# Decoder layer on one core: cross-attention keys and queries stacked per slot in 48 rows, two row tiles

## The chip, the cores and the metric

One core of a Trainium2 chip. The metric is the device time of one launch in microseconds (us). Three runs of the kernel before took 3350.82, 3353.17 and 3353.92 us, a median of 3353.17. The profiled execution took 3353.8 us, of which 3352.1 us are the span from the first instruction to the last.

## The reference, cut to what matters

A pre-norm decoder layer on 16 sequences of 128 tokens and 1024 features, fp32: self-attention, cross-attention over a context, feed-forward.

```python
x = x + attn(layernorm(x)); x = x + xattn(layernorm(x), ctx, ctx); x = x + ffn(layernorm(x))
# xattn: H = 16 heads, M = 4 superposed slots, dk = 16, projections of 1024 x 1024
scores = einsum('bhqdm,bhkdm->bhqkm', qh, kh) / sqrt(dk)
weights = softmax(scores, axis=3)
out = einsum('bhqkm,bhkdm->bhqdm', weights, vh)
```

There are 64 (head, slot) pairs. Each has its own score matrix over the 128 tokens of a sequence, with a contraction over only 16 features.

## The kernel before, in words

The layer runs in three phases, one after the other. The change is in the second, `cross_attention_phase` (L906). It goes over 4 blocks of 512 tokens (4 tiles of 128, a tile is one sequence) and, in each, over 8 groups of 128 projected features. A group holds 8 slots of 16 features. That makes 32 groups; they are software-pipelined in 33 steps: a step projects keys, queries and values of group n (`pieces`, 24 chunks of three matmuls of 128x512 in fp32r, a high and a low part of each operand) and does attention for group n-1.

The order of TensorE's work is written out by hand at the end of `step`: `scores(0)` first, the other three `scores(t)` between the pieces, with `turn_probs(t)` (transposes of the probabilities, L1261), `mix_values(t)` (L1281) and `project(t, half)` among them. The result of the projection stays in two banks and is split on ScalarE and VectorE into a high and a low half (`kh`, `kl`, `qh`, `ql`).

Scores need fp32 accuracy from fp32r operands: q·k is taken as qh·kh + qh·kl + ql·kh. For this the three products are put under one another in the contraction rows. Halves go out to HBM (`k_parts`, `q_parts`) and come back in another layout, all on SyncE's DMA queue: `stack_keys(a, part)` and `stack_queries(a, part)` (L1048 to L1056) for a = 0, 1, 2. Four pairs of slots (r = 0..3) each get a tile of 96 rows: 3 parts x (2 slots x 16 features). Keys lie block-diagonally: `kstack[96, pair, w, token]` holds slot w's 16 rows of each part in half w and zeros (a memset on GpSimd, once, L1143) in the other. Queries lie dense in `qstack[96, pair, token]`. One matmul (L1249) then gives both slots of a pair:

```python
ins = nc.tensor.matmul(s_ps[:, r * 2 * P:(r + 1) * 2 * P], qstack[:, r, t * P:(t + 1) * P],
                       kstack[:, r, :, t * P:(t + 1) * P], start=True, stop=True)
```

So `scores(t)` is 4 matmuls of 96 x 128 weights and 256 moving columns. `s_ps` spans two banks of 512 columns. After it VectorE takes the maximum per slot (L1512), ScalarE the exponentials in two halves of 4 slots (L1403), VectorE sums and inverses, GpSimd multiplies (L1163).

SyncE's order within a step: weights of the next group's first unit, `kh` to HBM, `kl` to HBM; then a wait for the last `scores` of the step (L1100, because `kstack` and `qstack` are single buffers) and for the landing of `kh`; `stack_keys(0)`; wait for `qh`, store it; `stack_keys(2)`; wait for `ql`, store it; `stack_keys(1)`; `stack_queries(0)`, `stack_queries(1)`; wait for the landing of `ql`; `stack_queries(2)`; then the weights of the second unit. Each `stack_keys` is two DMAs of 16 partitions and 128 KB, each `stack_queries` one DMA of 32 partitions and 256 KB. `scores(0)` of the next step waits for all nine (L1246, L1247).

The self-attention phase has two small TensorE blocks that matter as rows of comparison: L634 and L649. L649 (`mix_values` there) uses 32-row operands at partitions 0, 32, 64 and 96 in turn: 16 matmuls with 32 x 128 weights and 128 moving columns, plain fp32, of which the trace shows 32 in each of 32 blocks. L1281 in the cross-attention phase uses 128 x 32 weights with four output row groups, plain fp32.

Of the kernel before, what the change touches and what calls it, by code (L numbers as in the profile page):

```python
# [8 lines left out]
F32R = mybir.dt.float32r  # L9
# [4 lines left out]
P = 128  # L14
# [5 lines left out]
BT = TILES * P  # L20
# [16 lines left out]
DK = 16  # L37
# [8 lines left out]
def f32(ap):  # L46
    return ap.bitcast(F32)
# [858 lines left out]
def cross_attention_phase(nc, sems, ident, bias_qkv, eps, x1, ctxT, w_folded_hi, w_folded_lo, wo, k_parts, q_parts,  # L906
# [13 lines left out]
    PC = P // PAIRS  # L920
    PARTS = 3
    KSTACK = 16 * PARTS * 2
    QSTACK = 16 * PARTS
    STEPS = [CrossStep(n) for n in range(BLOCKS * CH + 1)]


# [7 lines left out]
    with ExitStack() as ctx:  # L934
        def sb(name, shape, dt=F32):
            return ctx.enter_context(nc.sbuf_tensor(name, shape, dt))
# [16 lines left out]
        kl = sb("ca_kl", [P, BT], F32R)  # L953
        qh = sb("ca_qh", [P, BT], F32R)
        ql = sb("ca_ql", [P, BT], F32R)
        kstack = sb("ca_kstack", [PARTS * PC, PAIRS, 2, BT], F32R)
        qstack = sb("ca_qstack", [PARTS * PC, PAIRS, BT], F32R)
        vT = sb("ca_vT", [P, BT])
        v = sb("ca_v", [P, TILES * PAIRS, VW])
        probs = sb("ca_probs", [P, 2, SLOTS, P])  # L960
# [67 lines left out]
        def _(sp):  # L1028
# [16 lines left out]
                    sp.wait_ge(c_split, b * KC + k)  # L1045
                sp.dma_start(raw_context(b, k), tile_of(ctxT, b * KC + k)).then_inc(c_loaded[k // 2], 16)

            def stack_keys(a, part):  # L1048
                by_slot = part.rearrange("(r w d) n -> w d r n", w=2, d=DK)
                for w in range(2):  # L1050
                    rows = slice(a * PC + w * DK, a * PC + (w + 1) * DK)
                    sp.dma_start(f32(kstack[rows, :, w]), by_slot[w]).then_inc(k_stacked, 16)

            def stack_queries(a, part):
                sp.dma_start(f32(qstack[a * PC:(a + 1) * PC]), part.rearrange("(r p) n -> p r n", p=PC)
                             ).then_inc(q_stacked, 16)  # L1056

            def store_x2(s, t):

# [16 lines left out]
            for s in STEPS:  # L1076
# [10 lines left out]
                if s.proj:  # L1087
                    sp.wait_ge(ow_split, s.n + 1)
                    sp.dma_start(owraw[:], tile_of(wo, s.g)).then_inc(owraw_loaded, 16)
                    next_weights(s, 0)  # L1090
                    sp.wait_ge(u_hi, s.n * 2 + 1)
                    sp.dma_start(k_parts[0], f32(kh[:])).then_inc(k_hi_stored, 16)
                    sp.wait_ge(u_free, s.n * U + 3)
                    sp.dma_start(k_parts[1], f32(kl[:])).then_inc(k_lo_stored, 16)
                    if after_closing:
                        load_acc(s.b, 1)
                        load_acc(s.b, 2)
                        load_acc(s.b, 3)
                    if s.attn:
                        sp.wait_ge(s_done, s.m * TILES + TILES)  # L1100
                    else:
                        sp.wait_ge(cleared, 1)
                    sp.wait_ge(k_hi_stored, s.n * 16 + 16)
                    stack_keys(0, k_parts[0])
                    sp.wait_ge(u_hi, s.n * 2 + 2)
                    sp.dma_start(q_parts[0], f32(qh[:])).then_inc(q_hi_stored, 16)
                    stack_keys(2, k_parts[0])
                    sp.wait_ge(u_free, s.n * U + 4)
                    sp.dma_start(q_parts[1], f32(ql[:])).then_inc(q_lo_stored, 16)
                    sp.wait_ge(k_lo_stored, s.n * 16 + 16)  # L1110
                    stack_keys(1, k_parts[1])
                    sp.wait_ge(q_hi_stored, s.n * 16 + 16)
                    stack_queries(0, q_parts[0])
                    stack_queries(1, q_parts[0])
                    sp.wait_ge(q_lo_stored, s.n * 16 + 16)
                    stack_queries(2, q_parts[1])
                    next_weights(s, 1)
# [22 lines left out]
        @block.gpsimd  # L1140
        def _(pool):
            pool.sem_inc(ow_split, 1)
            nc.gpsimd.memset(f32(kstack[:]), 0.0).then_inc(cleared, 1)  # L1143
            nc.gpsimd.memset(v[:], 0.0).then_inc(cleared, 1)

            def out_weights(s):
# [31 lines left out]
        def _(pe):  # L1178
# [19 lines left out]
            def step(s):  # L1198
# [42 lines left out]
                def scores(t):  # L1241
                    if not s.attn:
                        return
                    if t == 0:
                        pe.wait_ge(k_stacked, n * KSTACK)
                        pe.wait_ge(q_stacked, n * QSTACK)  # L1246
                    pe.wait_ge(exp_done, (m * TILES + t) * 2 + 2)  # L1247
                    for r in range(PAIRS):
                        ins = nc.tensor.matmul(s_ps[:, r * 2 * P:(r + 1) * 2 * P], qstack[:, r, t * P:(t + 1) * P],  # L1249
                                               kstack[:, r, :, t * P:(t + 1) * P], start=True, stop=True)  # L1250
                    ins.then_inc(s_done, 1)

                def turn_probs(t):
# [10 lines left out]
                def mix_values(t):  # L1264
# [12 lines left out]
                    pe.wait_ge(o_split, m * TILES + (t + 1))  # L1277
                    for w in range(2):
                        for r in range(PAIRS):
                            j = 2 * r + w  # L1280
                            ins = nc.tensor.matmul(o_ps[DP * r:DP * (r + 1), 0:P],  # L1281
                                                   v[:, t * PAIRS + r, DP * w:DP * (w + 1)],
                                                   probsT[:, j * P:(j + 1) * P], start=(w == 0), stop=(w == 1))
# [185 lines left out]
        def _(dve):  # L1469
# [10 lines left out]
            def step(s):  # L1480
# [19 lines left out]
                def place_v():  # L1500
                    if not s.attn:
                        return
                    dve.wait_ge(cleared, 2)
                    dve.wait_ge(v_turned, n)
                    nc.vector.tensor_copy(v[:].rearrange("p r (w x) -> p (r w) x", w=2)[:, :, 0:DK],
                                          t_ps[:, 0:BT].rearrange("p (s d) -> p s d", d=DK)).then_inc(v_placed, 1)
# [523 lines left out]
```

## Time and profile before

| | |
|---|---|
| profiled execution | 3353.8 us |
| its span | 3352.1 us |
| TensorE matmul busy | 3207.4 us, 96% |
| weight loads busy | 2580.7 us, 77% |
| VectorE, ScalarE, GpSimd busy | 42%, 36%, 49% |
| cross-attention scores (L1249) | 512 matmuls, 90.2 us busy, 17.5 us idle before them |
| DMA to `ca_kstack` | 192 of 128 KB, 3.4 us from issue to landing |
| DMA to `ca_qstack` | 96 of 256 KB, 5.4 us from issue to landing |

Matmuls are pipelined: one is recorded for 0.39 us while the next starts 0.23 us later. So the cost of a stretch of TensorE work is read from start to start, not from the durations. PE is the matmul, PEld the load of its weights. "[x <-issue]" behind a row is idle time of x us before it that ended when a wait in TensorE's own sequencer did.

### The profile page before, as it was taken

The page shows a single profiled execution, that of the slowest core. Times are in us where ns is not written, and L with a number is a line of the kernel's source. Part 1 is how long each engine was busy: PE and PEld are TensorE (multiplying, and loading weights), DVE is VectorE, ACT ScalarE, POOL GpSimd, SP SyncE. Part 2 cuts the span into 40 slices and gives each one's busy share as a digit, 9 for nine tenths or more (in the row PEclk, how much of TensorE's full clock was granted, in tenths as well). Part 3 has the DMA queues.
Part 4 walks back from the last instruction along what each step waited for, and adds up shares of the span by engine and source line. Part 5 has one row for each costly group of instructions (what it writes and reads, how often), then busy time and mean ns, then how long its engine had stood idle before and what let it go on. Part 6 is the DMA issues. An engine that isn't in the chain of part 4 may idle for free. (4 is left out here: it accounts for less than half of the span.)

```text
span 3352.1 us, 48808 instructions
## 1 busy us (share of the span) xinstructions
PE 3207.4 (96%) x18212; PEld 2580.7 (77%) x18212; DVE 1410.9 (42%) x2264; ACT 1210.5 (36%) x2433; POOL 1641.5 (49%) x1032
## 2 busy tenths in 40 slices
PE   7999999999999999999999969999999999998999
PEld 6777777778777777788888747777777777776787
DVE  3232242222242223233232235676666666664453
ACT  3233242232232322333333225565555555552100
POOL 4767667677676676765445333333333333331000
PEclk9999999999999999999999979999999999998999
DMA  5333344333344433435445256768768777765142
GB/s 190 101 119 114 124 138 146 119 114 105 126 131 147 131 103 116 144 101 201 150 133 162 93 208 213 230 200 256 219 204 254 232 211 246 236 189 206 66 143 76
DMA packets 176885, 536.23 MB, mean 160 GB/s; under 512 B 21704, under 2 KB 21832, under 8 KB 176728
## 3 DMA queue, kind: packets, MB, share of 16 engines
q1 hardware_dynamic: 174424, 525.65, 49.4%
q10 hardware_dynamic: 2304, 8.39, 0.6%
q8 instruction: 110, 1.80, 0.2%
q14 instruction: 47, 0.39, 0.0%
HBM read 433.29 MB, written 100.66 MB: 159 GB/s over the span
## 5 line engine op out<-in xcount | busy, mean ns | idle before, releaser
L53 PE MATMUL sa_u<-sa_ln_xh,sa_wh 128*128 128x512 f32 x1536 | 610.0, 397 | 38.0 <-POOL sa_wl L513 33.6
L54 PE MATMUL sa_u<-sa_ln_xl,sa_wh 128*128 128x512 f32 x1536 | 599.8, 390 | 0.0
L55 PE MATMUL sa_u<-sa_ln_xh,sa_wl 128*128 128x512 f32 x1536 | 599.1, 390 | 0.0
L513 POOL TENSOR_TENSOR sa_wl<-sa_wraw,sa_wh 128x1024 fp32r<-128x1024 f32 x192 | 459.9, 2400 | 170.3 <-ACT sa_wh L701 170.3
L563 POOL TENSOR_TENSOR sa_pl<-sa_praw,sa_ph 128x1024 fp32r<-128x1024 f32 x128 | 320.8, 2536 | 430.0 <-ACT sa_ph L755 430.0
L1163 POOL TENSOR_TENSOR ca_probs<-ca_probs,ca_inv 128x512 f32<-128x512 f32 x256 | 266.8, 1051 | 538.2 <-DVE ca_inv L1530 538.1
L850 DVE TENSOR_TENSOR sa_acc<-sa_pr,sa_acc 128x512 f32<-128x512 f32 x256 | 176.9, 691 | 774.5 <-PE sa_pr L55 774.5
L53 PE MATMUL sa_pr<-sa_ph,sa_oh 128*128 128x512 f32 x1024 | 403.0, 394 | 4.7 <-POOL sa_pl L563 4.4
L54 PE MATMUL sa_pr<-sa_pl,sa_oh 128*128 128x512 f32 x1024 | 404.2, 395 | 0.0
L55 PE MATMUL sa_pr<-sa_ph,sa_ol 128*128 128x512 f32 x1024 | 398.8, 389 | 0.0
L53 PEld LDWEIGHTS sa_u<-sa_ln_xh,sa_wh 128*128 128x128 f32 x1536 | 289.0, 188 | 114.2 <-POOL sa_wl L513 44.2
L55 PEld LDWEIGHTS sa_u<-sa_ln_xh,sa_wl 128*128 128x128 f32 x1536 | 289.1, 188 | 61.3
L54 PEld LDWEIGHTS sa_u<-sa_ln_xl,sa_wh 128*128 128x128 f32 x1536 | 289.4, 188 | 56.9
L719 ACT ACTIVATE sa_qT<-sa_u 128x512 f32<-128x512 f32 x128 | 76.5, 597 | 627.4 <-PE sa_u L55 627.4
L1403 ACT ACTIVATE ca_probs<-ca_s,ca_negtop 128x128 f32<-128x128 f32 x1024 | 286.7, 384 | 4.1
L842 DVE TENSOR_TENSOR sa_ol<-sa_s,sa_oh 128x512 fp32r<-128x512 f32 x32 | 22.1, 691 | 508.2 <-ACT sa_oh L767 508.2
L53 PEld LDWEIGHTS sa_pr<-sa_ph,sa_oh 128*128 128x128 f32 x1024 | 192.9, 188 | 50.4 <-POOL sa_pl L563 4.7
L55 PEld LDWEIGHTS sa_pr<-sa_ph,sa_ol 128*128 128x128 f32 x1024 | 192.8, 188 | 43.1
L54 PEld LDWEIGHTS sa_pr<-sa_pl,sa_oh 128*128 128x128 f32 x1024 | 193.2, 189 | 38.7
L701 ACT ACTIVATE sa_wh<-sa_wraw 128x1024 fp32r<-128x1024 f32 x192 | 202.0, 1052 | 17.8 <-DMA sa_wraw<-in_wqkv 17.8
L1521 DVE TENSOR_REDUCE ca_total<-ca_probs 128x4 f32<-128x512 f32 x256 | 172.7, 674 | 80.6 <-ACT ca_probs L1403 77.0
L1545 DVE TENSOR_TENSOR ca_acc<-ca_x,ca_acc 128x512 f32<-128x512 f32 x224 | 154.9, 691 | 122.3 <-PE ca_x L55 114.5
(215 smaller groups left out, 5778.8 us busy)
## 6 DMA issues: line engine op xcount, KB each, us to landing
sa_wraw<-in_wqkv SPq DMA_DIRECT2D x192, 512.0 KB, 3.7
sa_praw<-in_wproj SPq DMA_DIRECT2D x128, 512.0 KB, 3.7
three_wh<-w_folded_hi SPq DMA_DIRECT2D x96, 512.0 KB, 5.8
three_wl<-w_folded_lo SPq DMA_DIRECT2D x96, 512.0 KB, 6.8
ca_kstack<-k_parts SPq DMA_DIRECT2D x192, 128.0 KB, 3.4
ca_qstack<-q_parts SPq DMA_DIRECT2D x96, 256.0 KB, 5.4
ca_owraw<-in_wo SPq DMA_DIRECT2D x32, 512.0 KB, 3.8
sa_raw<-in_w_turned SPq DMA_DIRECT2D x24, 512.0 KB, 6.5
```

Source lines behind the costliest of these rows:

```text
L53: nc.tensor.matmul(out, ah, bh, start=(first and i == 0), stop=False)
L54: nc.tensor.matmul(out, ah, bl, start=False, stop=False)
L55: ins = nc.tensor.matmul(out, al, bh, start=False, stop=(last and i == len(parts) - 1))
L513: nc.gpsimd.tensor_tensor(wl[:, u % 3], wraw[:, u % 3], f32(wh[:, u % 3]), ALU.subtract).then_inc(w_split, 1)
L563: nc.gpsimd.tensor_tensor(pl[:, h], praw[:, h], f32(ph[:, h]), ALU.subtract).then_inc(p_split, 1)
L701: nc.scalar.activation(wh[:, u % 3], wraw[:, u % 3], ACT.Copy).then_inc(w_hi, 1)
L719: nc.scalar.activation(dst[u], u_ps[u % 2][:], ACT.Copy).then_inc(u_copied, 1)
L850: nc.vector.tensor_tensor(part, pr_ps[half][:], part, ALU.add).then_inc(pr_free, 1)
L1163: nc.gpsimd.tensor_tensor(probs[:, t % 2, js], probs[:, t % 2, js], inv[:, t % 2, js].unsqueeze(2).broadcast_to([P, SH, P]), ALU.mult).the ...
L1403: ins = nc.scalar.activation(probs[:, t % 2, j], s_ps[:, j * P:(j + 1) * P], ACT.Exp, scale=CROSS_SCALE, bias=negtop[:, j:j + 1])
L1521: nc.vector.tensor_reduce(total[:, t % 2, js], probs[:, t % 2, js], AX.X, ALU.add).then_inc(total_done, 1)
L1545: nc.vector.tensor_tensor(part, pr_bank(t, half)[:], part, ALU.add).then_inc(x_free, 1)
```

## The change

Keys and queries of each slot get 48 rows of their own (3 parts x 16 features): slot w of a pair sits at partitions 64w to 64w + 47, in `kstack` and in `qstack`. The zeros and their memset go, with SyncE's wait for it. A score matmul is one slot: 48 x 128 weights, 128 moving columns, from partition 0 or 64, with even slots written to the first bank of `s_ps` and odd ones to the second. There are 8 of them in a `scores(t)` in place of 4. `stack_queries` becomes two DMAs of 16 partitions and 128 KB, as the keys already have it; the keys' two keep number and size and write 8 KB in one piece per partition. The slot order in `s_ps` and behind it is all even, then all odd.

```diff
-    QSTACK = 16 * PARTS
+    QSTACK = 16 * PARTS * 2
+    ROWS = PARTS * DK
+    SLOT_TILE = 64
...
-        kstack = sb("ca_kstack", [PARTS * PC, PAIRS, 2, BT], F32R)
-        qstack = sb("ca_qstack", [PARTS * PC, PAIRS, BT], F32R)
+        kstack = sb("ca_kstack", [SLOT_TILE + ROWS, PAIRS, BT], F32R)
+        qstack = sb("ca_qstack", [SLOT_TILE + ROWS, PAIRS, BT], F32R)
...
-            def stack_keys(a, part):
+            def stack(dst, a, part, stacked):
                 by_slot = part.rearrange("(r w d) n -> w d r n", w=2, d=DK)
                 for w in range(2):
-                    rows = slice(a * PC + w * DK, a * PC + (w + 1) * DK)
-                    sp.dma_start(f32(kstack[rows, :, w]), by_slot[w]).then_inc(k_stacked, 16)
+                    rows = slice(w * SLOT_TILE + a * DK, w * SLOT_TILE + (a + 1) * DK)
+                    sp.dma_start(f32(dst[rows]), by_slot[w]).then_inc(stacked, 16)
+
+            def stack_keys(a, part):
+                stack(kstack, a, part, k_stacked)

             def stack_queries(a, part):
-                sp.dma_start(f32(qstack[a * PC:(a + 1) * PC]), part.rearrange("(r p) n -> p r n", p=PC)
-                             ).then_inc(q_stacked, 16)
+                stack(qstack, a, part, q_stacked)
...
-                    else:
-                        sp.wait_ge(cleared, 1)
...
-            nc.gpsimd.memset(f32(kstack[:]), 0.0).then_inc(cleared, 1)
...
                     for r in range(PAIRS):
-                        ins = nc.tensor.matmul(s_ps[:, r * 2 * P:(r + 1) * 2 * P], qstack[:, r, t * P:(t + 1) * P],
-                                               kstack[:, r, :, t * P:(t + 1) * P], start=True, stop=True)
+                        for w in range(2):
+                            rows = slice(w * SLOT_TILE, w * SLOT_TILE + ROWS)
+                            j = w * PAIRS + r
+                            ins = nc.tensor.matmul(s_ps[:, j * P:(j + 1) * P], qstack[rows, r, t * P:(t + 1) * P],
+                                                   kstack[rows, r, t * P:(t + 1) * P], start=True, stop=True)
...
-                            j = 2 * r + w
+                            j = w * PAIRS + r
```

## Rows read from the trace of the kernel before

**Rows 1.** Stretch: us, busy of PE, PEld, DVE, ACT, POOL; clock, DMA share, GB/s.
```profile
2018.00:3050.00 1032.00, 1010.17 (x6808) 795.43 (x6808) 686.57 (x1223) 569.05 (x1558) 371.66 (x311) 0.98 0.72 222
```

**Rows 2.** Groups by line of TensorE: busy, mean ns, idle before and what ended it.
```profile
L1249 PE MATMUL ca_s<-ca_kstack,ca_qstack 96*128 96x256 f32 x512 | 90.2, 299 | 17.5 <-issue 13.8 <-ACT ca_probs L1403 3.4
```

**Rows 3.** Timeline of PE, second step's scores(1), scores(2), scores(3): start, us, what.
```profile
2025.83 0.39 PE L55 MATMUL ca_u<-halves_h,three_wl 128*128 128x512 f32 x1
2026.05 0.64 PE L1249 MATMUL ca_s<-ca_kstack,ca_qstack 96*128 96x256 f32 x4
2026.53 0.40 PE L53 MATMUL ca_u<-halves_h,three_wh 128*128 128x512 f32 x1
2026.77 0.40 PE L54 MATMUL ca_u<-halves_l,three_wh 128*128 128x512 f32 x1
...
2031.54 0.74 PE L1249 MATMUL ca_s<-ca_kstack,ca_qstack 96*128 96x256 f32 x4
2032.12 0.40 PE L53 MATMUL ca_u<-ca_ln_xh,three_wh 128*128 128x512 f32 x1
...
2035.57 1.03 PE L1261 MATMUL ca_t<-ident,ca_probs 128*128 128x128 f32 x8
2036.36 0.72 PE L1249 MATMUL ca_s<-ca_kstack,ca_qstack 96*128 96x256 f32 x4
2036.92 0.40 PE L53 MATMUL ca_u<-halves_h,three_wh 128*128 128x512 f32 x1
```

**Rows 4.** Timeline of PE, one block of L649 between full-array matmuls.
```profile
1537.53 0.39 PE L55 MATMUL sa_u<-sa_ln_xh,sa_wl 128*128 128x512 f32 x1
...
1537.86 0.37 PE L649 MATMUL sa_vt<-sa_probsT,sa_v 32*128 32x128 f32 x1
...
1538.08 0.27 PE L649 MATMUL sa_vt<-sa_probsT,sa_v 32*128 32x128 f32 x1
...
1538.75 0.27 PE L649 MATMUL sa_vt<-sa_probsT,sa_v 32*128 32x128 f32 x1
1538.95 0.50 PE L53 MATMUL sa_u<-sa_ln_xh,sa_wh 128*128 128x512 f32 x1
1539.29 0.40 PE L54 MATMUL sa_u<-sa_ln_xl,sa_wh 128*128 128x512 f32 x1
```

**Rows 5.** Timeline of SP, the stacking behind ql of step 29: start, us, DMAs issued.
```profile
2913.99 0.42 SPq L1109 DMA_DIRECT2D q_parts<-ca_ql  x1
2914.46 0.92 SPq L1052 DMA_DIRECT2D ca_kstack<-k_parts  x2
2915.42 2.38 SPq L1055 DMA_DIRECT2D ca_qstack<-q_parts  x3
```

**Rows 6.** By tile, the DMAs of rows 5: ca_kstack x2, ca_qstack x3.
```profile
DMA to landing us min/median/max: 3.9/4.2/4.4
...
DMA to landing us min/median/max: 5.0/5.3/5.8
```

**Rows 7.** Stretches, columns as in rows 1: keys' pair, then queries, in that queue.
```profile
2917.25:2919.25 2.00, 2.00 (x14) 1.73 (x13) 0.69 (x1) 0.42 (x1) 0.00 (x0) 1.00 1.04 167
2919.50:2921.25 1.75, 1.75 (x21) 1.07 (x21) 0.81 (x2) 0.63 (x2) 0.00 (x0) 1.00 1.06 206
```

**Rows 8.** Timeline of PE: scores(0) behind the stacking of steps 29, 26 and 18.
```profile
2923.55 0.64 PE L1249 MATMUL ca_s<-ca_kstack,ca_qstack 96*128 96x256 f32 x4
...
2829.58 0.71 PE L1249 MATMUL ca_s<-ca_kstack,ca_qstack 96*128 96x256 f32 x4 [1.23 <-issue]
2830.13 0.39 PE L53 MATMUL ca_u<-ca_ch,three_wh 128*128 128x512 f32 x1
...
2571.16 0.71 PE L1249 MATMUL ca_s<-ca_kstack,ca_qstack 96*128 96x256 f32 x4 [1.67 <-issue]
```

**Rows 9.** Stretches, columns as in rows 1: behind the waits of 1.23 and 1.67 us.
```profile
2829.50:2833.00 3.50, 3.42 (x19) 2.98 (x20) 1.32 (x2) 1.38 (x6) 0.00 (x0) 1.00 1.04 410
2572.00:2575.30 3.30, 3.30 (x9) 2.51 (x8) 1.83 (x2) 2.10 (x9) 0.00 (x0) 0.50 1.03 420
```

More of the change, by code:

```diff
@@ L1502, in place_v @@
                         return
-                    dve.wait_ge(cleared, 2)
+                    dve.wait_ge(cleared, 1)
                     dve.wait_ge(v_turned, n)
```

## The prediction

> **What bounds the kernel now.** I read the page first (TensorE busy in 37 of 40 slices), then the stretch of the phase that changes: 1010 of 1032 us of it have a matmul in flight, so TensorE's stream sets the time [rows 1]. What it does beside streaming stands in the groups by line: 17.5 us idle before the scores, 3.4 of them on ScalarE in the last step, 13.8 on TensorE's own wait [rows 2]. The timeline places these at `scores(0)`, where the stacked keys and queries must have landed: 5.7 us in the first step and 8.1 us over eight later ones, two of which stand in [rows 8]. VectorE, ScalarE and GpSimd are busy 67%, 55% and 36% of the phase and nothing there is late but in the last step. So two things can move the time: the length of the four score blocks of a step, and the moment at which the last stacking DMA lands.
>
> **The score blocks on TensorE.** A block of four matmuls between full-array work costs, from the last L55 before it to the L54 behind it, 2026.77 - 2025.83 = 0.94 us [rows 3]; without a block that would be two starts of 0.23, so 0.48 us for four matmuls.
>
> The new block has eight matmuls in two row tiles. The trace has no block of two tiles, the nearest is L649 with four [rows 4]. Its 32 matmuls are eight rounds of four, one in each tile; the rows show the last tile of the rounds. From L55 to it 0.33 (0.10 above the usual 0.23); 0.22 to the second round (its weights can't be loaded ahead); then 0.67 for six rounds, 0.11 each; 0.20 from the last to L53; 0.34 from L53 to L54, 0.11 above the usual. Eight matmuls in two tiles are four rounds: 0.22 + 0.11 + 0.11 = 0.44 from first to last. Sum: 0.33 + 0.44 + 0.20 + 0.34 = 1.31, less 0.01 for two tiles fewer in a round, 1.30, against 0.94, so **+0.36 us** for a block between full-array matmuls. That is `scores(1)`, and `scores(0)` where it doesn't wait. Where it waits the entry is hidden: behind a wait the block now takes 0.55 to L53 [rows 8] and 0.23 on; it would take 0.44 + 0.01 + 0.20 + 0.34 = 0.99, so +0.21.
>
> `scores(2)` stands behind `mix_values`, itself a tiled block, and pays 0.58 to L53 today, not 0.48 [rows 3]: some of the change of tiling is paid already. 0.58 + 0.23 = 0.81 becomes 0.99: +0.18. `scores(3)` stands behind the transposes, 0.79 + 0.56 + 0.24 = 1.59 from the first of them to L54 [rows 3]; with the same 0.99 and an entry between 0 and 0.17 more I take 0.30 (0.19 to 0.36).
>
> A step: 0.21 + 0.36 + 0.18 + 0.30 = 1.05 us; 32 times: **+33 us**. All of it is on the path, since TensorE has no slack elsewhere in a step. Bounds: if entry and exit cost nothing, four rounds of 0.11 = 0.44 against 0.48, -0.04 x 128 = -5 us. If the two tiles didn't run side by side, eight times the 0.10 of a transpose with the same loads and columns (0.79 for eight, [rows 3]) makes 0.79 for 0.44: another 0.35 x 128 = +45, together +78. I take L649's own figures, since block and surroundings are alike; its plain fp32 is the one difference that speaks for the lower end.
>
> **The stacking.** The keys' six DMAs a step stay. The queries' three of 256 KB become six of 128 KB, with three issues more on SyncE at some 0.45 us [rows 5]. Behind them in that queue come the weights of the second unit, and the input tile or raw context; their first use is the ninth piece, behind eight pieces of three starts of 0.23 us [rows 3], 5.5 us after `scores(0)`, so 1.4 us later costs nothing. The queue is already backlogged there: the last query waits for the landing of `ql`, is issued at 2917.5 and lands 5.3 later, at 2922.8 [rows 5, 6]; 0.73 us on `scores(0)` starts unhindered [rows 8]. So in that backlog `ql` lands at 2917.5, the pair of keys (issued at 2914.5 and 2914.9) at 2918.3 and 2919.4, the queries at 2920.4, 2921.7 and 2922.8. So 256 KB as two DMAs of 16 partitions took 1.9 us and as one of 32 partitions 1.0 to 1.3. By rate the difference is smaller: 167 against 206 GB/s [rows 7]. The new queries are like the keys' pair. By the rate 786 KB take 4.7 us and not 3.8: +0.9. By the landings three pairs of 1.9 against 3.5: +2.2; but that 1.9 starts from the landing of a store in HBM and holds the difference between two kinds of landing, so the value is nearer to the rate. I take **+1.2 us**. Bounds: +2.2, and below nothing the rate that the same queue reaches with weights, 420 GB/s [rows 9], where 786 KB take 1.9 us, so -1.9.
>
> A block of scores(3) that ends 0.18 us later against what follows it (0.20 + 0.34 behind its last matmul, for 0.12 + 0.24) gives the chain 0.2 us back, because all of the chain hangs on `scores(3)`: the keys wait for it, and `qh` is drained behind its exponentials. So queries land 1.0 us later against TensorE. Read as in rows 5, 6 and 8, the 32 steps have these margins between landing and `scores(0)`: none in 12 steps (it waits already), 0.1 to 0.8 with mean 0.44 in 17, 1.3 to 1.6 in the three at a block's end. 12 x 1.0 + 17 x (1.0 - 0.44) = **+22 us**.
>
> Longer waits can cost the clock. Behind 1.23 us of waiting the granted clock stayed at 1.00, behind 1.67 it was 0.50 for 3.3 us [rows 8, 9], which is 1.2 and not 2.4 GHz and gave up half of that, 1.7 us. Of the new waits only two cross from one to the other (0.86 and 1.23, in steps 22 and 26, plus 1.0); the many of 1.0 to 1.3 don't: **+3 us**.
>
> The rule that bears on the stacking: the Trainium skill, "SBUF — State Buffer", Door 1, says that a transfer's rate goes with the ports that its partitions reach, four ports for 16 partitions at 27 GB/s each, and that partitions 32 apart share a port while 64 apart don't. Partitions 0 to 31 and 32 to 63, the first two query DMAs of today, then share eight ports, which gives 1.2 us each and agrees with the 1.2 measured; the new pairs reach the other half too. By that rule six in flight could use all sixteen and need 1.8 us instead of 3.5, or, one after another, 7.2. Which it is hangs on how many run at once, and no row shows it for halves 64 apart.
>
> **Cheap edits.** The memset on GpSimd (3.5 us once, at the start) and SyncE's wait for it lie beside the first projections; they are worth nothing. Slot order: the reduce, the exponentials and the copies keep their shapes, so nothing.
>
> **Sum.** 3353.8 (profiled execution) + 33 + 22 + 3 = 3412; it stands 0.6 above the median, so **3411 us**, 1.7% slower.
>
> **Rivals.**
> First, *the queries land no later* (0): only the blocks count. 3353 + 33 less some 2 of the present waits: 3384. For it: the rate of 167 is a short stretch, and six DMAs may spread better than two. Against it: the landings.
>
> Second, *they land sooner* by up to 1.9 us, because the two halves go to different parts of the memory: the 8.1 us of later waits go, with them two dips of the clock (3.4, that of [rows 9] and one behind a wait of 3.2 us), and 1.8 in the first step; the blocks cost 3 more, since `scores(0)` waits nowhere. 3353 + 36 - 13 = 3376. The port rule above, with all six in flight, gives the same.
>
> Third, *the stacking is worse*: +2.2 by the landings, 2.0 after the give-back: 12 x 2.0 + 17 x 1.56 + 3 x 0.5 = 52, and every one of the 12 has over 1.67 us of wait, so some 12 dips of 1.7 = 20. 3353 + 33 + 52 + 20 = 3458.
>
> Fourth, *the two tiles don't run side by side* (the change doesn't do what it says): +45 on my sum, 3456.
>
> Fifth, on the other side, *a change of tiling costs nothing for fp32r*: entry and exit in rows 4 belong to plain fp32, and the new blocks take 0.44 for 0.48: -5. For it: the transposes, plain fp32 on the full array, also lengthen what stands behind them (0.56 for 0.48). Against it: `scores(2)`, fp32r behind a tiled block, is 0.10 longer than `scores(1)`. With queries landing as now that is 3348 and with the second rival 3335; it decides from the point where entry and exit together are below 0.1 us.
>
> **Chances.** Forecast 0.50, first and second rival 0.11 each, third 0.14, fourth 0.05, fifth 0.09, of which half ends over 0.2% faster (the stacking sooner or the waits shorter) and half within. What a measurement of this kernel can tell from no change is about 0.2%, 7 us. Faster 0.05, within 0.04, slower 0.91. The range runs from 3374, the second rival, to 3458, the third; it leaves out the fifth, and the upper part of the third and the fourth, together 0.2.
>
> **What will show it.** In the timeline behind the change: L55 to L54 around `scores(1)` near 1.30 (0.9 would be the fifth rival, 1.6 the fourth); starts of a pair within 0.02 us and 0.11 from pair to pair. The idle before the scores: about 40 us in place of 17.5, most at `scores(0)` with 0.5 to 2.2 us (under 10: first or second rival, over 65: the third). Queries landing 0.9 to 1.5 us later behind `ql` than the 5.3 of today. The prediction is wrong if the blocks come out below 1.1 us or if the wait before `scores(0)` shrinks.

## The result, and the profile after

The changed kernel took 3405.32 us (median of 4 runs, 3396.97 to 3408.32) against 3353.55 us of the kernel before beside it (4 runs, 3350.82 to 3354.65). The ratio is 1.015, 95% interval 1.0134 to 1.0166: slower by 52 us. The forecast was 3411 us, in a range from 3374 to 3458. The same kernel, run again later beside the experiments, came to 3407.21 us, ratio 1.0165 (1.0151 to 1.0179).

The profiled execution took 3407.0 us, its span 3405.2. These are TensorE's groups by line that answer to [rows 2] (busy, mean ns | idle before and what ended it), with the transposes of the probabilities below:

```profile
L1253 PE MATMUL ca_s<-ca_kstack,ca_qstack 48*128 48x128 f32 x1024 | 87.9, 292 | 33.2 <-issue 30.0 <-ACT ca_probs L1407 3.2
...
L1265 PE MATMUL ca_t<-ident,ca_probs 128*128 128x128 f32 x1024 | 135.4, 276 | 2.6 <-issue 1.4 <-POOL ca_probs L1164 1.0
```

Before, the transposes had this line:

```profile
L1261 PE MATMUL ca_t<-ident,ca_probs 128*128 128x128 f32 x1024 | 135.5, 276 | 5.6 <-issue 4.4 <-POOL ca_probs L1163 1.2
```

Twice as many score matmuls are busy for no longer than before (87.9 us for 90.2). Busy time does not show the cost. The idle time shows a part of it: TensorE's own wait before the scores went from 13.8 to 30.0 us. The rest is in the starts. Here is TensorE's timeline of `scores(1)`, `scores(2)` and `scores(3)` of the second step, which answers to [rows 3] (start, us, what):

```profile
2064.29 0.39 PE L55 MATMUL ca_u<-halves_h,three_wl 128*128 128x512 f32 x1
2064.61 0.66 PE L1253 MATMUL ca_s<-ca_kstack,ca_qstack 48*128 48x128 f32 x8
2065.20 0.50 PE L53 MATMUL ca_u<-halves_h,three_wh 128*128 128x512 f32 x1
2065.54 0.39 PE L54 MATMUL ca_u<-halves_l,three_wh 128*128 128x512 f32 x1
...
2069.75 0.65 PE L1285 MATMUL ca_o_ps<-ca_probsT,ca_v 128*32 128x128 f32 x16
2070.32 0.66 PE L1253 MATMUL ca_s<-ca_kstack,ca_qstack 48*128 48x128 f32 x8
2070.91 0.50 PE L53 MATMUL ca_u<-ca_ln_xh,three_wh 128*128 128x512 f32 x1
...
2074.47 1.03 PE L1265 MATMUL ca_t<-ident,ca_probs 128*128 128x128 f32 x8
2075.43 0.66 PE L1253 MATMUL ca_s<-ca_kstack,ca_qstack 48*128 48x128 f32 x8
2076.03 0.50 PE L53 MATMUL ca_u<-halves_h,three_wh 128*128 128x512 f32 x1
2076.36 0.39 PE L54 MATMUL ca_u<-halves_l,three_wh 128*128 128x512 f32 x1
```

`scores(1)` now takes 2065.54 - 2064.29 = 1.25 us from L55 to L54, where it took 0.94. The eight matmuls alone are quick. Their starts come in four pairs, 0.39 from the first to the last. But the way in is 0.32 (a plain start is 0.23), from the last pair to L53 pass another 0.20, and L53 to L54 takes 0.34. Behind the value block (L1285) and behind the transposes (L1265) the exits are the same.

The other part is the stacking. This is SyncE's timeline of the third step, which answers to [rows 5]:

```profile
2081.13 0.41 SPq L1111 DMA_DIRECT2D q_parts<-ca_ql  x1
2081.59 0.90 SPq L1054 DMA_DIRECT2D ca_kstack<-k_parts  x2
2082.53 4.31 SPq L1054 DMA_DIRECT2D ca_qstack<-q_parts  x6
```

Over the 32 steps the last query lands 4.60 us behind the last key (mean), where it was 3.51. The last key itself lands a little sooner behind `ql` than before (1.72 for 1.99), and `ql` behind the issue of `qh` (5.24 for 5.35), so the whole chain, from the issue of `qh` to the last query, grew by 0.72 us, from 10.85 to 11.57.

What that does to TensorE stands in the longest wait, that of `scores(0)` in step 18, which was 1.67 us in [rows 8]:

```profile
2594.09 0.40 PE L55 MATMUL ca_o_ps<-ca_owh,ca_ol 128*128 128x512 f32 x1
2598.59 1.12 PE L1253 MATMUL ca_s<-ca_kstack,ca_qstack 48*128 48x128 f32 x8 [4.10 <-issue]
```

and in the stretches around and behind it, with the phase as a whole ahead of them, as in [rows 1] and [rows 9] (us, busy of PE, PEld, DVE, ACT, POOL; clock, DMA share, GB/s):

```profile
2018.00:3100.00 1082.00, 1044.77 (x7297) 802.32 (x7298) 682.14 (x1220) 568.66 (x1557) 372.11 (x311) 0.98 0.72 212
...
2597.85:2604.60 6.75, 6.01 (x22) 4.95 (x23) 1.92 (x2) 2.39 (x9) 0.00 (x0) 0.50 0.95 379
2604.70:2625.00 20.30, 20.30 (x143) 15.94 (x142) 14.93 (x29) 11.47 (x34) 9.27 (x8) 1.00 0.39 131
```

The granted clock was at 0.50, which is 1.2 GHz, from the last 0.7 us of the 4.10 us of waiting on, for 6.75 us, and then at 1.00 again.

From the first `scores(0)` to that of step 32 it is 998.9 us before and 1048.3 after, +49.4. The waits before `scores(0)` in between grew from 8.3 to 23.9 (+15.6). Stretches at half clock, without the parts of them in which TensorE waited, grew from 10.8 to 23.2 us; half of the difference is lost time (+6.2). The transposes wait 2.5 less in between. What is left, 49.4 - 15.6 - 6.2 + 2.5 = 30.1, is the score blocks.

### The profile page after: what moved, and what is told of

Read it like the earlier page. It is cut to its first block and busy times, and to the rows that moved or that the text cites. A ratio compares the mean times of both kernels' runs of the same rounds, so it can differ in the third digit from the quotient of the medians.

```text
span 3405.2 us, 49926 instructions
## 1 busy us (share of the span) xinstructions
PE 3246.0 (95%) x18724; PEld 2590.9 (76%) x18724; DVE 1405.8 (41%) x2264; ACT 1211.5 (36%) x2433; POOL 1639.0 (48%) x1031
## 5 line engine op out<-in xcount | busy, mean ns | idle before, releaser
L53 PE MATMUL sa_u<-sa_ln_xh,sa_wh 128*128 128x512 f32 x1536 | 610.1, 397 | 37.9 <-POOL sa_wl L513 33.6
L54 PE MATMUL sa_u<-sa_ln_xl,sa_wh 128*128 128x512 f32 x1536 | 599.9, 391 | 0.0
L55 PE MATMUL sa_u<-sa_ln_xh,sa_wl 128*128 128x512 f32 x1536 | 599.5, 390 | 0.0
L53 PE MATMUL sa_pr<-sa_ph,sa_oh 128*128 128x512 f32 x1024 | 402.5, 393 | 5.2 <-POOL sa_pl L563 4.4
L54 PE MATMUL sa_pr<-sa_pl,sa_oh 128*128 128x512 f32 x1024 | 404.0, 395 | 0.0
L55 PE MATMUL sa_pr<-sa_ph,sa_ol 128*128 128x512 f32 x1024 | 398.6, 389 | 0.0
L53 PEld LDWEIGHTS sa_u<-sa_ln_xh,sa_wh 128*128 128x128 f32 x1536 | 289.2, 188 | 114.0 <-POOL sa_wl L513 44.2
L55 PEld LDWEIGHTS sa_u<-sa_ln_xh,sa_wl 128*128 128x128 f32 x1536 | 289.2, 188 | 61.4
L54 PEld LDWEIGHTS sa_u<-sa_ln_xl,sa_wh 128*128 128x128 f32 x1536 | 289.4, 188 | 57.2
L53 PEld LDWEIGHTS sa_pr<-sa_ph,sa_oh 128*128 128x128 f32 x1024 | 192.8, 188 | 50.8 <-POOL sa_pl L563 4.7
L55 PEld LDWEIGHTS sa_pr<-sa_ph,sa_ol 128*128 128x128 f32 x1024 | 192.6, 188 | 42.9
L54 PEld LDWEIGHTS sa_pr<-sa_pl,sa_oh 128*128 128x128 f32 x1024 | 193.0, 188 | 38.6
```

What stands on the lines that cost most here:

```text
L53: nc.tensor.matmul(out, ah, bh, start=(first and i == 0), stop=False)
L54: nc.tensor.matmul(out, ah, bl, start=False, stop=False)
L55: ins = nc.tensor.matmul(out, al, bh, start=False, stop=(last and i == len(parts) - 1))
```

## The experiments

My theory was that two separate costs add up: the entry into the tiles and the way out of them, and the queries' stacking in twice as many DMAs. The main rival was that only one of the two is real. All ratios below are to the kernel before on the same chip (3350.8 to 3352.1 us).

**The pieces without the tiles.** The kernel before, its queries in six DMAs:

```diff
-                sp.dma_start(f32(qstack[a * PC:(a + 1) * PC]), part...).then_inc(q_stacked, 16)
+                by_slot = part.rearrange("(r w d) n -> w d r n", w=2, d=DK)
+                for w in range(2):
+                    rows = slice(a * PC + w * DK, a * PC + (w + 1) * DK)
+                    sp.dma_start(f32(qstack[rows]), by_slot[w]).then_inc(q_stacked, 16)
```

> The kernel before, with its score blocks and layouts untouched; only the queries' three stacking DMAs of 32 partitions (256 KB) become six of 16 partitions (128 KB), as in the kernel after, though with the two halves 16 partitions apart and not 64. My theory (the pieces make the queries late): score blocks stay at 0.94 us, the last query lands 0.7 to 1.1 us later behind the last key than the 3.5 us of before, the idle before the scores grows from 17.5 to some 30 us, and a dip of the clock or two more comes with it; 3353 + 15 to 25, so 3368 to 3378 us. Rival (the score blocks are the whole cost, a later landing is hidden): 3353 within 0.2%. Rival (the cost of the pieces lies in the halves being 64 partitions apart): the same 3353, with the last query 3.5 us behind the last key.

It took 3389.1 us, ratio 1.0111 (1.0096 to 1.0127), so +38 and not 15 to 25. The block is unchanged. TensorE's group by line, and the queries' DMAs (KB each, median us from issue to landing; 256 KB and 5.4 before):

```profile
L1251 PE MATMUL ca_s<-ca_kstack,ca_qstack 96*128 96x256 f32 x512 | 92.2, 303 | 47.6 <-issue 44.2 <-ACT ca_probs L1405 3.3
```

```profile
ca_qstack<-q_parts SPq DMA_DIRECT2D x192, 128.0 KB, 5.4
```

The last query landed 4.86 us behind the last key, 1.35 later than before. I had said 0.7 to 1.1, and 30 us of idle before the scores where it is 47.6. A later landing is not hidden, and 32 steps multiply each tenth of it. Halves next to one another cost no less than halves 64 apart (a piece lands 0.88 us behind the last one here and 0.82 in the kernel after, means), so the distance is not what made the pieces dear.

**The tiles without the pieces.** The kernel after, its queries again in three DMAs of 32 partitions, so that their rows no longer match the keys':

```diff
-                stack(qstack, a, part, q_stacked)
+                sp.dma_start(f32(qstack[a * PC:(a + 1) * PC]), part.rearrange("(r p) n -> p r n", p=PC)
+                             ).then_inc(q_stacked, 16)
```

> The kernel after, with its two row tiles, but the queries come in three DMAs of 32 partitions (256 KB) as before, so their rows hold other features than the keys' rows: the layout of the queries is left out, and the scores aren't those of the reference. Work on every engine and bytes moved are those of the kernel after. My theory (blocks and waits add up): L55 to L54 around scores(1) stays at 1.26 us, the last query lands some 3.5 us behind the last key and not 4.6, the waits before scores(0) come to 8 to 10 us over steps 2 to 32 and not 25, no clock dips beyond those of before; 3353 + 29 to 33 - 2, so 3378 to 3386 us. Rival (the waits are nearly all of the 52 us, and longer blocks are given back by shorter waits): 3353 to 3362. Rival (the waits come from the longer blocks, not from the pieces): 3405, with the waits at 25 us.

It took 3377.54 us, ratio 1.0079 (1.0065 to 1.0093), +27. TensorE's group by line:

```profile
L1258 PE MATMUL ca_s<-ca_kstack,ca_qstack 48*128 48x128 f32 x1024 | 86.5, 289 | 15.5 <-issue 12.3 <-ACT ca_probs L1412 3.2
```

The idle is below that of before, and of the stretches at half clock between the first and the last `scores(0)` only the one behind the first is left. With waits, clock and transposes taken out as above, the blocks cost +29.9 us. So the tiles make +27 of the +52 to +55, each against the kernel before on its own chip, and the pieces the rest, 25 to 28. The pieces cost 38 alone and 25 to 28 behind tiles. With tiles they put the last query 0.98 us further behind the last key (4.60 for 3.62), alone 1.35 (4.86 for 3.51). With tiles TensorE also works a little longer between the last matmul of `scores(3)` and `scores(0)` (15.1 us for 14.9, waits left out), which gives the queries time. How much each of the two counts was not separated.

**Eight matmuls without tiles.** The kernel before, each matmul of 256 columns split in two:

```diff
-                        ins = nc.tensor.matmul(s_ps[:, r * 2 * P:(r + 1) * 2 * P], qstack[:, r, t * P:(t + 1) * P],
-                                               kstack[:, r, :, t * P:(t + 1) * P], start=True, stop=True)
+                        for w in range(2):
+                            j = 2 * r + w
+                            ins = nc.tensor.matmul(s_ps[:, j * P:(j + 1) * P], qstack[:, r, t * P:(t + 1) * P],
+                                                   kstack[:, r, w, t * P:(t + 1) * P], start=True, stop=True)
```

> The kernel before, with each score matmul of 256 columns split into two of 128 on the same full array: eight weight loads in place of four, as many columns, no row tiles. My theory (with 128 columns the loading of weights sets the pace, some 0.11 us each, since the rounds of two tiles came at 0.11 too): eight matmuls take 8 x 0.11 = 0.87 us where four took 0.48, +0.39 a block, of which 128 blocks make +45 to 50: 3398 to 3403 us. So the side-by-side run of two tiles would win back what the smaller matmuls cost and no more. Rival (loads are hidden beside streaming, columns set the pace): the block stays 0.94 us and the time 3353 within 0.2%.

It took 3401.47 us, ratio 1.0153 (1.0138 to 1.0169), +50.6, as my theory had it. TensorE's timeline of one block:

```profile
2028.48 0.39 PE L55 MATMUL ca_u<-halves_h,three_wl 128*128 128x512 f32 x1
2028.71 1.01 PE L1251 MATMUL ca_s<-ca_kstack,ca_qstack 96*128 96x128 f32 x8
2029.55 0.44 PE L53 MATMUL ca_u<-halves_h,three_wh 128*128 128x512 f32 x1
2029.83 0.39 PE L54 MATMUL ca_u<-halves_l,three_wh 128*128 128x512 f32 x1
```

From L55 to L54 it is 1.35, with the eight starts 0.10 apart (0.73 from first to last). In two tiles they take 0.39 and the surroundings cost more: 1.25. So the run in pairs is real, saves 0.34 a block against eight on the full array, and gives 0.24 of it back. Neither reaches the 0.94 of four matmuls with 256 columns, which start 0.12 apart: twice the columns for 0.02 us more.

**One tile's matmuls in a row.** The kernel after, the loops over the two tiles and the four pairs exchanged:

```diff
-                    for r in range(PAIRS):
-                        for w in range(2):
+                    for w in range(2):
+                        for r in range(PAIRS):
```

> The kernel after with the eight matmuls of a score block in another order: the four of one row tile, then the four of the other, in place of pairs. Loads, columns, DMAs and the tiling are the same. My theory (two tiles run side by side only if the order lets them; the loads of one tile follow at 0.11 us): first to last of a block 0.39 becomes 0.8, +0.40 to 0.44 on each of 128 blocks, 3405 + 51 to 56, so 3456 to 3461 us. Rival (TensorE takes the other tile's matmuls ahead, or the pace is that of the columns alone): first to last stays at 0.39 and the time at 3405.

My theory fell. TensorE's timeline of a block:

```profile
2031.25 0.39 PE L55 MATMUL ca_u<-halves_h,three_wl 128*128 128x512 f32 x1
2031.57 0.67 PE L1253 MATMUL ca_s<-ca_kstack,ca_qstack 48*128 48x128 f32 x8
2032.17 0.50 PE L53 MATMUL ca_u<-halves_h,three_wh 128*128 128x512 f32 x1
2032.51 0.40 PE L54 MATMUL ca_u<-halves_l,three_wh 128*128 128x512 f32 x1
```

Eight matmuls in 0.67, not over 1: the starts are again in pairs, 0.013 us apart. The records do not name the tile. Matmuls of one tile start 0.11 apart in [rows 4], and 0.10 to 0.11 on the full array, so by the pace TensorE started the second tile's first matmul with the first tile's, though three stood between them in the program. That is an inference: no run has a block in one tile of 64 rows alone. The time was 3416.65 us, ratio 1.0191 (1.0176 to 1.0206). The 9 to 11 us above the kernel after are not in the blocks (0.012 x 128 = 1.5 us). They are in the waits: 41.6 us of idle before the scores, where the kernel after showed 30.0 and, run again, 32.4. Its chain is 12.10 us against 11.57 and 11.68, with the same DMAs: a query piece lands 0.89 us behind the last one, for 0.82 and 0.84 (means). Why is open.

**The change of tiling by itself.** The kernel before, with one small tiled matmul ahead of each block:

```diff
+                    nc.tensor.matmul(s_ps[:, 0:P], qstack[0:48, 0, t * P:(t + 1) * P],
+                                     kstack[0:48, 0, 0, t * P:(t + 1) * P], start=True, stop=True)
                     for r in range(PAIRS):
```

> The kernel before with one small matmul more ahead of each score block: 48 rows, 128 columns, in a row tile, into columns that the block then overwrites. It prices the entry into a tile and the way back to the full array. My theory: +0.09 into the tile, and behind it the first full-array matmul starts 0.20 later with its 0.11 load in the open, so some 0.4 a block, less behind the value blocks, which are tiled already: 128 x 0.3 to 0.4 = +38 to 51, 3390 to 3402 us. Rival (a change of tiling costs nothing, only the load counts): 128 x 0.11 = +14, 3365 us.

It took 3399.45 us, ratio 1.0144 (1.0129 to 1.0158), +48.6. TensorE's timeline:

```profile
2032.10 0.39 PE L55 MATMUL ca_u<-halves_h,three_wl 128*128 128x512 f32 x1
2032.41 0.33 PE L1248 MATMUL ca_s<-ca_kstack,ca_qstack 48*128 48x128 f32 x1
2032.67 0.76 PE L1251 MATMUL ca_s<-ca_kstack,ca_qstack 96*128 96x256 f32 x4
2033.26 0.39 PE L53 MATMUL ca_u<-halves_h,three_wh 128*128 128x512 f32 x1
2033.50 0.40 PE L54 MATMUL ca_u<-halves_l,three_wh 128*128 128x512 f32 x1
```

L55 to L54 is 1.40 for 0.94: one tiled matmul of 128 columns costs 0.46 us, where one more load on the full array costs 0.10. Behind the values, which are tiled already, it costs 0.25 (medians, 1.64 for 1.39 from the first of them to L54). The fifth rival, that a change of tiling is free, is refuted.

**Where the stacks land.** First the kernel before with the second and third part exchanged, so that neighbours in the queue go to different halves of the partitions:

```diff
-                    stack_keys(2, k_parts[0])
+                    stack_keys(1, k_parts[0])
...
-                    stack_queries(1, q_parts[0])
+                    stack_queries(2, q_parts[0])
```

> The kernel before, with the second and third part of the stacks exchanged: the DMAs keep their sources, sizes and order of issue, but the second pair of keys goes to partitions 64 to 95 where it went to 32 to 63, and the third to 32 to 63; the queries' second goes to 64 to 95 and their third to 32 to 63. The sum over parts is the same in another order. Theory A (transfers to the lower and to the upper half of the partitions share no way into the memory, so neighbours in the queue overlap): the last query lands 0.5 to 1.2 us sooner, the waits before scores(0) fall from 8 to some 2 to 4 us, a dip or two of the clock goes; 3340 to 3348 us. Theory B (the queue's pace doesn't hang on where they land): chain 3.5 us as before, 3353 within 0.2%.

It took 3348.71 us, ratio 0.9996 (0.9987 to 1.0005): no change. The last query landed 3.58 us behind the last key (3.51 before). That is Theory B.

Then the rows themselves spread, each part of the queries and of the keys in every fourth row of 128, in the kernel before (the cut below shows the queries) and in the kernel after:

```diff
-                sp.dma_start(f32(qstack[a * PC:(a + 1) * PC]), part...
+                sp.dma_start(f32(qstack[a:P:PAIRS]), part...
```

> The kernel before; the three parts of the stacks lie in rows 4 apart (row 4 i + a holds row i of part a; every fourth row stays zero), so that a query DMA of 32 partitions reaches over all 128 and a key DMA of 16 over 64. Sources, bytes, number and order of DMAs and the four matmuls of a block are those of before. Theory A (a DMA's rate goes with how far its partitions lie spread; a store of 256 KB from all 128 lands 0.62 us behind its neighbour, a query piece into 32 neighbouring partitions 1.22): last key to last query 3.5 us becomes 1.8 to 2.4, no wait is left before scores(0) but in the first step, no dip of the clock behind one: 3351 - 8 - 1.8 to 3.4, so 3338 to 3342 us. Theory B (the rate goes with the number of partitions or of 2 KB rows, wherever they lie): chain and time of before, 3351 within 0.2%.

> The kernel after with the same spread of rows: in each 64-row tile row 4 i + a holds row i of part a (every fourth row zero), so that one DMA of 32 partitions brings a part of both slots: three key and three query DMAs a step in place of six and six. The score blocks stay eight matmuls in two row tiles, now of 64 rows. Theory A (spread partitions raise the rate): blocks cost 29 to 31 us as before, the waits before scores(0) all but go, with them the dips: 3351 + 30 - 8 - 1.8 to 3.4, so 3366 to 3372 us. Theory B (the rate goes with the number of partitions): the queries as in the kernel before, the keys' three DMAs some 0.3 us a pair sooner: 3374 to 3380 us.

With the blocks of before it took 3349.94 us, ratio 0.9991 (0.9982 to 1.0001): no change in time. But the DMAs became quicker. TensorE's groups by line, and the keys' and queries' DMAs (3.4 and 5.4 us to landing before):

```profile
L1262 PE MATMUL ca_t<-ident,ca_probs 128*128 128x128 f32 x1024 | 134.8, 275 | 11.7 <-issue 10.4 <-POOL ca_probs L1164 1.2
...
L1250 PE MATMUL ca_s<-ca_kstack,ca_qstack 128*128 128x256 f32 x512 | 90.1, 299 | 9.9 <-issue 6.4 <-ACT ca_probs L1404 3.5
```

```profile
ca_kstack<-k_parts SPq DMA_DIRECT2D x192, 128.0 KB, 2.8
ca_qstack<-q_parts SPq DMA_DIRECT2D x96, 256.0 KB, 3.5
```

The chain from `qh`'s issue to the last query fell from 10.85 to 9.88 us and the waits before the scores by 7.4 us. Theory A's own sign did not come, though. The last query lands 3.70 us behind the last key, not 1.8 to 2.4: the second piece lands 0.93 behind the first for 1.22, but the third 1.80 behind the second for 1.22 (medians). What became shorter lies ahead of it: the last key lands 1.27 us behind `ql` for 1.99, and `ql` 4.92 behind the issue of `qh` for 5.35. The gain did not reach the end: the transposes, idle for 4.4 us before, now wait 10.4. Two timelines show the chain behind one of these waits, VectorE's and then TensorE's:

```profile
2671.08 0.69 DVE L1561 BATCH_NORM_STATS2 ca_ln_stats<-ca_ln_x 128x6 f32<-128x512 f32 x1 [3.24 <-DMA ca_ln_x<-x]
2671.69 0.67 DVE L1506 COPY ca_v<-ca_t 128x512 f32<-128x512 f32 x1
2672.28 0.68 DVE L1522 TENSOR_REDUCE ca_total<-ca_probs 128x4 f32<-128x512 f32 x1
```

```profile
2675.39 0.84 PE L1262 MATMUL ca_t<-ident,ca_probs 128*128 128x128 f32 x6 [1.80 <-issue]
```

VectorE stands in order behind the statistics of the next block's input tile and waits 3.24 us for its DMA. Behind it come the values' copy and the sums of the probabilities, on which GpSimd and then the transposes hang. That load stands in SyncE's queue behind 1 MB of weights.

With the blocks of after it took 3370.81 us, ratio 1.0057 (1.0044 to 1.0069): no wait at all before `scores(0)` of steps 2 to 32, no stretch at half clock behind any of them, and the blocks at +29.1 us by the same account as above. So this is the change with the stacking's cost taken away, and it still loses 20 us.

**The input tile first.** The load moved ahead of the weights, with the spread rows and without:

```diff
-                    next_weights(s, 1)
                 if s.more and 1 <= s.g <= TILES:
                     sp.wait_ge(ln.turned, s.b * ln.GROUPS + ln.GROUPS)
                     load(s.b + 1, ln.x, ln.loaded, [s.g - 1])
+                if s.proj:
+                    next_weights(s, 1)
```

> The kernel with rows 4 apart, and in the 12 steps that load a tile of the next block's input, that load is issued ahead of the second unit's weights (two loads of 512 KB) and not behind them. Theory: with rows 4 apart the waits before scores(0) fell by 7.4 us (13.8 to 6.4) and 6.0 of them came back before the transposes (4.4 to 10.4), because VectorE stands in order behind the statistics of that tile and so is late with the sums of the probabilities; the tile lands 3.2 to 5.6 us after scores(0). Landing about 2 us sooner, it takes the idle before the transposes to 1 to 4 us: 3350 - 6 to 9, so 3341 to 3344 us, and under 3351 by 0.2 to 0.3%. Rival (the wait before the transposes has another cause, VectorE's own order of work): 3350, the idle at 10. Rival (the weights, now later, are waited for): over 3350, with idle before L53 of the second unit.

> The kernel before with that one exchange alone: the input tile's load ahead of the second unit's weights. Theory: the 4.4 us idle before the transposes fall to 1 to 2, and some of it comes back before scores(0), whose stacks land no sooner: 3351 - 1 to 3, so 3348 to 3350 us, hardly to be told from 3351. Rival (the input tile alone is what was late): 3347 or less. Rival (the weights are waited for): over 3353.

With both edits it took 3339.56 us (3335.91 to 3342.09), ratio 0.9961 (0.9947 to 0.9975): it beats both kernels, by 12.6 us that of before. TensorE's groups:

```profile
L1263 PE MATMUL ca_t<-ident,ca_probs 128*128 128x128 f32 x1024 | 134.5, 275 | 3.5 <-issue 2.2 <-POOL ca_probs L1165 1.2
...
L1251 PE MATMUL ca_s<-ca_kstack,ca_qstack 128*128 128x256 f32 x512 | 89.9, 298 | 9.8 <-issue 6.4 <-ACT ca_probs L1405 3.4
```

The transposes' wait fell from 10.4 to 2.2 us, as expected, and the scores' stayed at 6.4, of which 4.8 are the first step's. VectorE's waits for that tile behind the first `scores(0)`, twelve of 1.2 to 3.6 us with the spread rows alone, fell to two of 0.2. Of the stretches at half clock between the first and the last `scores(0)` only the one behind the first is left. Against the kernel before that is 7.4 + 2.2 us less of waits, 1.3 more of waits at the output projection's L53 (for VectorE, not for weights) and 3.9 less for the clock, 12.2 of the 12.6 measured. The exchange alone took 3347.64 us, ratio 0.9987 (0.9978 to 0.9996), between its theory's range and its rival's, so it decides neither: the transposes' wait fell by the same 2.2 us, and the waits before the scores by 1.8, where I had expected some to come back.

**The kernel after again**, on the same chip as these:

> The kernel after once more, beside the other kernels on their chip. If the 11 us by which its kernel with the order tile by tile was slower (3416.65 against 3405.32) are a matter of the chip or of how the waits happen to fall and not of the order, it comes out between 3405 and 3416 here, with the idle before the scores between 33 and 45 us; if they are the price of the order, 3403 to 3407 with 33 us.

3407.21 us and 32.4 us of idle before the scores lie close to the second reading, the price of the order, so the 9 us to the order tile by tile may be that kernel's own. That isn't shown: it ran on another chip, and its interval (from 1.0176) and this one (to 1.0179) overlap.

## Why the prediction was right, point by point

**The score blocks**, forecast +33 us, came out at +29 to 30 by three kernels (30.1, and 29.5 in its second run; 29.9; 29.1). Medians: `scores(1)` +0.31 for the forecast 0.36, `scores(2)` +0.12 for 0.18, `scores(3)` +0.31 for 0.30, and `scores(0)` behind a wait +0.15 for 0.21. By these starts 31 steps make 28 to 33, as `scores(0)` waits or not. The entry and the exits of plain fp32 in [rows 4] held for fp32r within 0.01 us. Too large was the second round: it starts 0.16 behind the first and not 0.22, so that first to last is 0.39 and not 0.44. L649 puts four tiles in a round, and this block two; whether that is the reason no run shows.

The Trainium skill, "TensorEngine Tiling (Array Packing)", Key Properties, says that a change of tiling mode drains TensorE. The trace agrees in that each change has a price, and gives the price that the page does not: 0.46 us for one tiled matmul between full-array ones, its own load included.

**The stacking**, forecast +22 us, came out at +15.6 before `scores(0)`. The queries did land later behind the last key, by 1.1 us for the forecast 1.2. From that the forecast took 0.2 that the longer way out of `scores(3)` was to give back, which left 1.0. Counted from the last matmul of `scores(3)`, the last query lands after 15.56 us for 14.66 (+0.90), and TensorE's own work up to `scores(0)`, waits left out, takes 15.12 for 14.86 (+0.26; means of 31 steps). So the queries came 0.64 us later against TensorE, 0.76 in the second run of the kernel after, and the 1.0 is the term of mine that was mis-sized. TensorE's work grew as forecast, but the issue of `qh` moved back with it, to 3.97 us behind the last score matmul from 3.79, so most of that gave nothing back. What made up for it is that the last key landed 0.27 sooner behind `ql` (0.17 in the second run) and `ql` 0.11 sooner behind the issue of `qh`, which the prediction didn't have and no run explains.

The delay also fell unevenly. I had each step shifted alike, so that 29 of 32 steps would wait; 19 do (11 before), and four waits alone hold 4.10 + 3.56 + 3.23 + 2.74 = 13.6 of the 23.9 us. The first three stand in steps 18, 10 and 26, which had the longest waits before, too (1.67, 3.17 and 1.23). In these steps SyncE issues three loads of accumulator tiles, 512 KB each, ahead of the keys, which the prediction didn't mention. This is its timeline in step 18 of the kernel after:

```profile
2578.02 1.43 SPq L1043 DMA_DIRECT2D ca_acc<-x  x3
2581.33 0.80 SPq L1054 DMA_DIRECT2D ca_kstack<-k_parts  x2
2583.38 0.34 SPq L1108 DMA_DIRECT2D q_parts<-ca_qh  x1
...
2590.57 2.65 SPq L1054 DMA_DIRECT2D ca_qstack<-q_parts  x6
```

From the issue of `qh` to the landing of `ql` it is 7.9 to 8.5 us in these three steps, and mostly 4.8 in the others. That the loads are the cause is argued from the order of the queue; no run moved them. The whole chain differs from step to step by up to 5 us (9.8 to 15.1), where the mean shift is 0.7. So a mean margin is a poor guide to the waits of single steps.

**The clock**, forecast +3, came out at +6.2. The dips stand at the longest waits, as forecast, but those are longer (3.23, 3.56 and 4.10 us), and the clock stayed down for 6.8 us at each where [rows 9] has 3.3. The forecast read from two rows that waits beyond some point between 1.23 and 1.67 us cost the clock. That did not hold: at 1.88 and 2.74 us of wait it stayed at 1.00, while in the second run of the kernel after it fell for 3.4 us at 1.62, 2.72 and 3.22. So the length of a wait alone doesn't tell whether the clock falls, or for how long.

**The sum.** 30 + 16 + 6, less 2.5 that the transposes wait less, is the +49.4 of the 53.1 us between the two spans. Another 4.3 lie ahead of the first `scores(0)`, at 2022.7 for 2018.4; of these 0.4 are its own wait, and 2.9 lie in the self-attention phase, where nothing was changed and whose end falls anywhere from 1962 to 1966 us in the thirteen traces. Behind the last `scores(0)` it is 0.5 less. Against the forecast's 3412 for the profiled execution that is 3 less for the blocks, 6 less for the queries, 2.5 less for the transposes, 3 more for the clock, 4 more ahead and 0.5 less behind, 3407 for the 3407.0 measured. For what the change itself did the forecast was some 9 us too high, and that the 4 us ahead, which no run ties to the change, make up for half of it is luck. Of the signs, the idle before the scores came to 33.2 us for about 40, and the queries landed 0.8 us later behind `ql` (6.33 for 5.50, means) for 0.9 to 1.5.

**The rivals.** That the queries land no later is refuted by the chain, and its time, 3384, is close to what the kernel with wide queries took (3377.5). That they land sooner is refuted too, and neither 1.8 nor 7.2 us, between which the prediction left the six pieces, came: the last of them lands 4.60 us behind the last key. By the port rule of the Trainium skill, "SBUF — State Buffer", Door 1, rows 4 apart reach twice the ports, which by estimate halves the time of 256 KB. In the kernel with spread rows the second query piece landed 0.93 us behind the first for 1.22 (medians): the direction is right, the size is not. Exchanging the parts of two DMAs did nothing. That the tiles don't run side by side, with 0.79 us for a block, is refuted by the 0.39 from first to last, and that a change of tiling is free by the 0.46 us. The range began at 3374 for the second rival, whose own sum says 3376; nothing hangs on it.

## What to carry to other kernels

A tiled block between full-array matmuls pays for its way in and out, here 0.09 us ahead of it and 0.19 behind it, so a small tiled block can cost more than it saves. In [rows 4], where 32 matmuls stand together, the same is paid once. Halving the columns of a matmul to get rid of multiplied zeros bought nothing here, since on the full array a matmul of 128 columns started 0.10 us behind the last and one of 256 only 0.12. When a wait is shortened, look in the trace for the next one on the same path before calling the edit worthless: the quicker stacks were worth nothing until the input tile behind them was moved as well.

## What the runs showed of the hardware

Eight matmuls of two row tiles started in pairs, 0.39 to 0.40 us from first to last, whether the program took the tiles in turn or all four of one first; I had expected 0.8 for the second order. DMAs of 256 KB into 32 partitions 4 apart took 3.5 us from issue to landing, and 5.4 into 32 neighbouring ones, on the same queue with the same bytes; the keys' DMAs ahead of them were spread too. Yet the last of them came no sooner behind the keys (3.70 us for 3.51). A query DMA split into two of 16 partitions made the last query land 1.0 to 1.35 us later behind the last key.
